# Decoder kernel: scan rows shared by two engines, paired spreads, residual at the first down products, low halves on GpSimd

## Time and profile before

| | us |
|---|---|
| time, median of 3 runs | 3944.65 |
| the profiled execution: its time, and its span | 3938.74, 3937.0 |
| PE busy, DVE busy | 3515.4 (89%), 3180.0 (81%) |
| ACT busy, POOL busy | 1623.4 (41%), 1347.1 (34%) |
| mean granted TensorE clock | 0.941 of full speed |

### The profile page before, as it was taken

How to read it: one execution, slowest core, us unless ns; L and a number is a source line. 1 busy time by engine, 2 the same in 40 slices (tenths; PEclk the granted TensorE clock), 3 DMA queues, 4 the chain that set the end, 5 groups by cost and what they waited for, 6 DMA issues and landing times. The chain is left out here.

```text
span 3937.0 us, 41370 instructions
## 1 busy us (share of the span) xinstructions
PE 3515.4 (89%) x15406; PEld 1471.1 (37%) x15406; DVE 3180.0 (81%) x2733; ACT 1623.4 (41%) x2201; POOL 1347.1 (34%) x493
## 2 busy tenths in 40 slices
PE   5777779989999979999999989998999989977998
PEld 1222243334333443334333443334433443324444
DVE  5999569888999869788999869888999869795333
ACT  5666343224655353224655343224655353213001
POOL 3455304362344304352344304352344304351000
PEclk9888899999899999989999999999899999988999
DMA  6678402221233302221233302221233302110322
GB/s 231 244 278 299 174 17 73 76 72 57 87 100 104 132 27 73 76 65 64 88 104 101 132 27 73 76 69 61 87 100 105 132 27 73 57 41 17 104 97 73
DMA packets 105430, 382.94 MB, mean 97 GB/s; under 512 B 14224, under 2 KB 27920, under 8 KB 102800
## 3 DMA queue, kind: packets, MB, share of 16 engines
q1 hardware_dynamic: 83632, 342.57, 25.5%
q10 hardware_dynamic: 21600, 37.73, 3.4%
HBM read 290.80 MB, written 64.32 MB: 90 GB/s over the span
## 5 line engine op out<-in xcount | busy, mean ns | idle before, releaser
L300 PE MATMUL ps<-r,ring 128*128 128x512 bf16 (+1 forms) x2040 | 780.8, 383 | 0.0
L297 PE MATMUL ps<-xr,ring 128*128 128x512 bf16 x1568 | 613.8, 391 | 0.3 <-PEq L1853 0.3
L301 PE MATMUL ps<-xr,ring 128*128 128x512 bf16 x1568 | 610.8, 390 | 0.0
L297 PE MATMUL ps<-r,ring 128*128 128x512 bf16 (+2 forms) x1384 | 546.8, 396 | 50.2 <-DVE xc L1107 17.9
L301 PE MATMUL ps<-r,ring 128*128 128x512 bf16 (+2 forms) x1384 | 545.5, 395 | 0.0
L1159 POOL TENSOR_TENSOR hh<-hh,bc 128x2048 f32<-128x2048 f32 x72 | 334.8, 4650 | 512.3 <-DVE hh L1069 512.3
L1159 POOL TENSOR_TENSOR bc<-bc 128x2048 f32<-128x2048 f32 x64 | 304.3, 4755 | 344.5 <-DVE bc L1069 344.5
L1159 POOL TENSOR_TENSOR r<-r,bc 128x2048 f32<-128x2048 f32 x56 | 261.3, 4667 | 298.5 <-DVE r L1069 298.5
L1069 DVE TENSOR_TENSOR_SCAN hh<-da,hh 128x2048 f32<-128x2048 f32 x72 | 325.6, 4523 | 1.2
L1110 DVE TENSOR_TENSOR xc<-xc,ps 128x512 f32<-128x512 f32 x176 | 119.5, 679 | 226.7 <-PE ps L301 226.7
L1069 DVE TENSOR_TENSOR_SCAN bc<-da,bc 128x2048 f32<-128x2048 f32 x64 | 296.3, 4630 | 0.5
(11 more groups left out here) (271 smaller groups left out, 6552.5 us busy)
## 6 DMA issues: line engine op xcount, KB each, us to landing
ring<-wsplit SPq DMA_DIRECT2D x216, 768.0 KB, 4.3
r<-wstream SPq DMA_DIRECT2D x54, 768.0 KB, 7.5
ring<-wsplit SPq DMA_DIRECT2D x76, 512.0 KB, 4.0
wsplit<-ring SPq DMA_DIRECT2D x38, 768.0 KB, 4.8
da<-r ACTq DMA_DIRECT2D x360, 63.9 KB, 2.1
wsplit<-r SPq DMA_DIRECT2D x14, 768.0 KB, 5.0
r<-wstream SPq DMA_DIRECT2D x19, 512.0 KB, 6.3
r<-xT SPq DMA_DIRECT2D x7, 1024.0 KB, 4.8
```

Source lines behind the costliest of these rows:

```text
L297: mm = pe.matmul(out, w_hi, x_hi, start=start, stop=False)
L300: pe.matmul(out, w_hi, x_lo, start=False, stop=False)
L301: return pe.matmul(out, w_lo, x_hi, start=False, stop=stop)
```

## The change

Four parts, in the words of the code:

- In the first scan (`halved`) POOL multiplies two of the four groups of a block with C, and DVE the other two, right after `inputs(step + 1)`. `reduce_quad` waits for both.
- In the expert stage every fourth spread of dt*x (`early_spread`: blocks 4, 8, ... 28) goes to `y_bank`, one step earlier, directly behind the spread of the block before it. `inputs_of` moves from `step % 4 == 2` to `step % 4 == 1`.
- In ffn and expert stages the first four down products are added to the residual `xr` instead of copied; ln2 and ln5 leave out `sums` and its wait.
- `ffn_xlo` is made by POOL at the end of `norm_and_steps`, a quarter after each quarter of `scaled`, instead of by DVE at the start of the ffn stage.

```diff
+        own_read, halved = sem("own_read"), not tiles
+        def early_spread(s):
+            return gated and s % 4 == 0 and 4 <= s < blocks
+        def input_bank(s):
+            return y_bank if early_spread(s) else dtx_bank
             def spread_dtx(s):
-                if s >= 1:
-                    pe.wait_ge(inp, s)
+                if early_spread(s):
+                    if s >= 8:
+                        pe.wait_ge(yout, s // 4 - 1)
+                elif s >= 1:
+                    pe.wait_ge(inp, s - 1 if early_spread(s - 1) else s)
...
-                pe.matmul(dtx_bank, k.headmean[at, :], source, start=True, stop=True).then_inc(dtx_mm, 1)
+                pe.matmul(input_bank(s), k.headmean[at, :], source, start=True, stop=True).then_inc(dtx_mm, 1)
             def reduce_quad(j):
                 pe.wait_ge(read, 4 * j + 4)
+                if early_spread(4 * j + 4):
+                    pe.wait_ge(inp, 4 * j + 5)
+                if halved:
+                    pe.wait_ge(own_read, 4 * j + 4)
...
-            if tiles and not gated:
-                pe.wait_ge(xsplit, KM)
...
-                if 2 <= step + 1 < blocks:
+                if 2 <= step + 1 < blocks and not early_spread(step + 1):
                     spread_dtx(step + 1)
+                if early_spread(step + 2):
+                    spread_dtx(step + 2)
...
-                    dve.tensor_copy(k.xc[:, m, :], down_bank(p)).then_inc(taken, 1)
+                    dve.tensor_tensor(k.xc[:, m, :], k.xr[:, m, :], down_bank(p), ALU.add).then_inc(taken, 1)
...
-            if tiles and not gated:
-                for c in range(KM):
-                    low(dve, xlo[:, c, :], k.xr[:, c, :]).then_inc(xsplit, 1)
...
+                if halved and step < blocks:
+                    dve.wait_ge(scanned, step + 1)
+                    own = quartet(step)[:, GRP // 2:GRP, :]
+                    dve.tensor_tensor(own, own, k.out_rows[:, GRP // 2:GRP, :], ALU.mult).then_inc(own_read, 1)
...
-                if which == 0 and step % 4 == 2 and step + 2 < blocks:
+                if which == 0 and step % 4 == (1 if gated else 2) and step // 4 * 4 + 4 < blocks:
                     inputs_of(step // 4 + 1)
...
-                pool.tensor_tensor(quartet(s), quartet(s), k.out_rows, ALU.mult).then_inc(read, 1)
+                rows = slice(0, GRP // 2 if halved else GRP)
+                pool.tensor_tensor(quartet(s)[:, rows, :], quartet(s)[:, rows, :], k.out_rows[:, rows, :], ALU.mult).then_inc(read, 1)
...
 class LayerNorm:
     def means(self, pe):
-                pe.wait_ge(self.res, 2 * h + c // 2 + 1)
+                if not self.summed:
+                    pe.wait_ge(self.res, 2 * h + c // 2 + 1)
     def sums(self, dve):
+        if self.summed:
+            return
...
 def norm_and_steps(...):
         def _(pool):
             s.build_spread(pool)
+            for half in range(2):
+                for pair in range(2):
+                    pool.wait_ge(norm.out, 2 * half + pair + 1)
+                    part = lambda region: region[:, 2 * pair:2 * pair + 2, half * HT:(half + 1) * HT]
+                    pool.tensor_tensor(part(k.ffn_xlo), part(k.xr), part(high(k.xr)), ALU.subtract)
```

More of the change, by code:

```diff
@@ L587, in second_preparation @@
         if store is not None:
-            norm = LayerNorm(k, "ln5", k.xc, k.xr, [k.ps[:, 6 + h, 0:HT] for h in range(2)], [k.ps[:, 6 + h, HT:T] for h in range(2)], True)
+            norm = LayerNorm(k, "ln5", k.xc, k.xr, [k.ps[:, 6 + h, 0:HT] for h in range(2)], [k.ps[:, 6 + h, HT:T] for h in range(2)], True, True)
         gates_in = k.dt0
@@ L819, in hidden_and_scan @@
         gate_mm, up_mm, th, silu, hid, weighted = [sem(n) for n in ("gate_mm", "up_mm", "th", "silu", "hid", "weighted")]
-        hidlo, xsplit, down, taken = [sem(n) for n in ("hidlo", "xsplit", "down", "taken")]
+        hidlo, down, taken = [sem(n) for n in ("hidlo", "down", "taken")]
         dt_mm, dtx_mm, decay, others = [sem(n) for n in ("dt_mm", "dtx_mm", "decay", "others")]
@@ L1058, in inputs @@
                     dve.wait_ge(reduced, (s - NB) // 4 + 1)
-                dve.tensor_tensor(quartet(s), dtx_bank[:, None, :].broadcast_to([P, GRP, T]), k.in_rows, ALU.mult).then_inc(inp, 1)
+                dve.tensor_tensor(quartet(s), input_bank(s)[:, None, :].broadcast_to([P, GRP, T]), k.in_rows, ALU.mult).then_inc(inp, 1)
             def inputs_of(j):
@@ L1158, in _, with __init__ @@
                 pool.wait_ge(scanned, s + 1)
-                pool.tensor_tensor(quartet(s), quartet(s), k.out_rows, ALU.mult).then_inc(read, 1)
+                rows = slice(0, GRP // 2 if halved else GRP)
+                pool.tensor_tensor(quartet(s)[:, rows, :], quartet(s)[:, rows, :], k.out_rows[:, rows, :], ALU.mult).then_inc(read, 1)
 class LayerNorm:
-    def __init__(self, k, tag, parts, residual, mean_bank, var_bank, shared=False):
+    def __init__(self, k, tag, parts, residual, mean_bank, var_bank, shared=False, summed=False):
+        self.summed = summed
         self.shared = shared
@@ L1235, in scaled, with layer_norm @@
                                   ALU.mult).then_inc(self.out, 1)
-def layer_norm(nc, k, tag, parts, slots_end, last, store=None, load=None, split=None, ranges=(), residual=None):
+def layer_norm(nc, k, tag, parts, slots_end, last, store=None, load=None, split=None, ranges=(), residual=None, summed=False):
     with ExitStack() as ctx:
@@ L1245, in layer_norm @@
         norm = LayerNorm(k, tag, parts, k.xr if residual is None else residual, [k.ps[:, 4 + h, 0:HT] for h in range(2)],
-                         [k.ps[:, 6 + h, 0:HT] for h in range(2)])
+                         [k.ps[:, 6 + h, 0:HT] for h in range(2)], summed=summed)
         blk = ctx.enter_context(nc.Block())
@@ L2355, in sequence @@
                     hidden_and_scan(nc, k, "ffn", FFN_TILES, W_FFN, 1, False, last, end=W_PROJ + 3 if ahead else None)
-                    layer_norm(nc, k, "ln2", k.xc, W_MIX, last, load=(k.xn, xT[b + 1]) if ahead else None,
+                    layer_norm(nc, k, "ln2", k.xc, W_MIX, last, summed=True, load=(k.xn, xT[b + 1]) if ahead else None,
                                split=k.xn_lo if ahead else None)
@@ L2364, in sequence @@
                     if not ahead:
-                        layer_norm(nc, k, "ln5", k.xc, last, last, store=out[b])
+                        layer_norm(nc, k, "ln5", k.xc, last, last, store=out[b], summed=True)
                 if ahead:
```

## The result

The changed kernel takes a median of 3919.68 us in four runs (3912.42 to 3927.57), the kernel before 3946.62 beside it: ratio 0.9937, 95% interval 0.9918 to 0.9957. Measured a second time it takes 3922.38 us beside 3941.38 for the kernel before: 0.9947 (0.9929 to 0.9966). (Times are medians; the ratios are worked out from all runs, so they differ a little from the quotient of two medians.) The forecast was 3908, with 3890 to 3931: the time lies inside, 12 us above the forecast. By its parts, two terms came out as forecast and two brought about half and 0.6 of it.

A forecast was written before the change was run, and what follows sets the result against it. It took the first scan as bound by DVE's and POOL's SBUF work end to end, the expert stage by PE with DVE close behind. Terms -20 - 23 - 4 + 10 = -37 us gave 3908 us from the median, range 3890 to 3931.

The forecast's parts named there:

- First scan: First scan, 32 blocks: POOL's multiply shared with DVE shortens each block; -20 us, bounds -31 and +5.
- 32 x 1.1 is 35 us: First scan: a gain of 1.1 us read in single blocks, taken for all 32, 35 us before deductions.
- The third taken off for what is late next: First scan: the 30 us gain cut by a third because weight loads would not shrink with the steps, leaving -20 us.
- The rival in which the split leaves only 4 us: First scan: the weight split bounds it, so it gains 4 us instead of 20; 3924 us, chance 0.20.
- Paired spreads: Three expert stages, seven pairs each: two spreads cost PE the time of one; 3 x 7.6 = -23 us, bounds -29 and 0.
- each of the six waits falls by 1.05 and by what PE was ahead: Expert stage: DVE's six waits for a spread, 9.8 us, shrink to 2.2 us, saving 7.6 us a stage.
- the slower rival: Expert stages: the early spread stops PE at the wait for `inputs_of` in every quad, +136 us; 4067 us, chance 0.04.
- the one in which pairs bring little: Expert stages: the two matmuls don't run side by side, or DVE limits at once; -3 for -23, 3928 us, chance 0.10.
- Residual: Four ln2 and the last ln5: without `sums` PE's means start about 0.75 us sooner; -4 us, bounds -1 and -7.
- Low halves: Four ln1 stages: POOL's instructions exclude DVE's last six, 2.5 us longer each; +10 us, bounds 0 and +14.
- the rival in which they are free: ln1: POOL's four instructions fall into gaps of DVE and cost nothing; 3898 us, chance 0.05.

The follow-up runs named there:

- short loads: The changed kernel with each load of weights in the first scan cut to 384 of up to 1536 columns, output not the reference's: 3916.64 us in one execution.
- the gap filled: The changed kernel with ffn_xlo's low halves back on DVE, plus 32 useless matmuls at the end of PE's order in ln1: 3916.15 us, ratio 0.9926.

## Why the prediction was right, and where its terms were not

**First scan: -20 forecast, -10.5 measured** (327 to 330 us against 337 to 340; -11.7 in the profiled execution). What it said of the single block holds. The changed kernel's timeline:

```profile
295.58 2.36 POOL L1176 TENSOR_TENSOR hh<-hh,bc 128x1024 f32<-128x1024 f32 x1 [6.13 <-DVE hh L1084]
...
298.94 4.41 DVE L1084 TENSOR_TENSOR_SCAN bc<-da,bc 128x2048 f32<-128x2048 f32 x1
303.28 1.73 DVE L265 TENSOR_TENSOR r<-r 128x1536 bf16<-128x1536 f32 x1
303.43 3.79 POOL L1176 TENSOR_TENSOR bc<-bc 128x1024 f32<-128x1024 f32 x1 [5.49 <-DVE bc L1084]
305.07 2.29 DVE L1074 TENSOR_TENSOR bc<-ps,bc 128x2048 f32<-128x2048 f32 x1
307.28 1.22 DVE L1142 TENSOR_TENSOR bc<-bc 128x1024 f32<-128x1024 f32 x1
308.41 4.42 DVE L1084 TENSOR_TENSOR_SCAN bc<-da,bc 128x2048 f32<-128x2048 f32 x1
```

From scan to scan (298.94 to 308.41) it is 9.47 us with a piece of low half, 9.33 forecast, and 7.85 without one (144.14 to 151.99), 7.68 forecast; scans take 4.41 throughout. By the Trainium skill (SBUF — State Buffer, section "SBUF: two separate sides") DVE with two inputs in SBUF and POOL exclude each other for a whole instruction; the trace agrees, since POOL's half takes 3.79 us behind line 265 and 2.36 at 295.58, where DVE is in `inputs`.

The step that failed is "32 x 1.1 is 35 us": it carried a pattern read in two blocks to all. There are 31 intervals from the end of one scan to the end of the next. Taken one by one in the two traces, 20 of them are 1.0 us shorter (0.98 to 1.03); the other eleven are together 9.7 us longer. With 1.1 us that the tail gains, as forecast, this is the 11.7.

Two things are in the eleven. The first is work. In the trace of before, DVE stands behind POOL's multiply in 28 of the 31 intervals, but not always in the scan: 18 of the 32 scans are longer than 5.5 us; seven times line 1063 in front of a scan took the wait (2.80 to 3.05 us in place of 0.68), and three times line 265 did (here 5.36 and 3.98 us in place of 1.73). In three intervals nothing did, since DVE had waited for its spread until POOL was done or nearly so, as here from 284.95:

```profile
284.95 2.29 DVE L1059 TENSOR_TENSOR hh<-ps,bc 128x2048 f32<-128x2048 f32 x1 [3.91 <-PE ps L894]
287.81 4.42 DVE L1069 TENSOR_TENSOR_SCAN hh<-da,hh 128x2048 f32<-128x2048 f32 x1
343.19 5.36 DVE L265 TENSOR_TENSOR ring<-r,ring 128x1536 bf16<-128x1536 f32 x1 [0.86 <-ACT ring L260]
357.55 3.98 DVE L265 TENSOR_TENSOR ring<-r,ring 128x1536 bf16<-128x1536 f32 x1 [2.27 <-ACT ring L260]
```

In those three the own half adds 1.1 us and removes nothing. 28 x 1.0 - 3 x 1.1 is 25 us in place of 35. `finish_y` was hidden in three of its eight blocks only (before scans of 6.15, 5.80 and 6.15 us), so it costs 2 and not 5, and the own half of the last block costs DVE another 1.2: 22 us of DVE's work, with 21.3 measured, where the forecast had 30. The second is waits, below. The groups of the stage (count, busy, mean ns, idle before) show the trade. Before:

```profile
L1069 DVE TENSOR_TENSOR_SCAN bc<-da,bc 128x2048 f32<-128x2048 f32 x10 | 58.1, 5807 | 0.5
L265 DVE TENSOR_TENSOR ring<-r,ring 128x1536 bf16<-128x1536 f32 (+3 forms) x16 | 33.6, 2100 | 3.9 <-ACT ring L260 3.9
L1063 DVE TENSOR_TENSOR ctxTs<-r 128x512 f32<-128x512 f32 x8 | 20.8, 2606 | 0.3 <-PEq L486 0.3
```

After:

```profile
L1084 DVE TENSOR_TENSOR_SCAN bc<-da,bc 128x2048 f32<-128x2048 f32 x10 | 44.1, 4412 | 0.0
L1074 DVE TENSOR_TENSOR hh<-ps,bc 128x2048 f32<-128x2048 f32 x12 | 27.4, 2286 | 18.9 <-PE ps L905 18.9
L265 DVE TENSOR_TENSOR ring<-r,ring 128x1536 bf16<-128x1536 f32 (+3 forms) x16 | 25.9, 1621 | 10.6 <-ACT ring L260 10.6
L1078 DVE TENSOR_TENSOR ctxTs<-r 128x512 f32<-128x512 f32 x8 | 5.5, 682 | 0.3 <-PEq L486 0.3
L1142 DVE TENSOR_TENSOR bc<-bc 128x1024 f32<-128x1024 f32 x10 | 12.1, 1210 | 0.0
```

DVE's busy time falls by 21.3 us (312.39 to 291.09) and its idle time grows by 9.6: waits for the spread 12.5 to 19.6 us, for ACT's half of the split 3.9 to 10.6, for the reduction 8.4 to 6.0. Five intervals lose 1.4 to 3.4 us each by them, three to the spread and two to ACT. The third taken off for what is late next (10 us) was thus right in size, and 21.3 less 9.6 is the 11.7. The loads are a part of it (short loads: 3 to 7 us); how the rest divides between PE's order and ACT wasn't settled, except that the bank of the spread isn't it. The rival in which the split leaves only 4 us holds in part: DVE's waits for ACT's half grew by 6.7 us, but ACT's own waits for loads, which it named, fell from 9.1 + 2.4 us to 6.3 + 2.1.

**Paired spreads: -23 forecast, -13.8 measured** (4.8, 4.4 and 4.7). A pair costs 1.06 us as the earlier trace rows said, here from 1183.43 to the product behind it:

```profile
1183.43 1.13 PE L905 MATMUL ps<-ctxTs,squares_sb 32*128 32x512 f32 x4 [0.15 <-issue]
1184.49 0.40 PE L297 MATMUL ps<-xr,ring 128*128 128x512 bf16 x1
```

and PE's four steps take 40.07 us, 40.1 forecast. The failing step is "each of the six waits falls by 1.05 and by what PE was ahead". DVE's waits after the first blocks are now

```profile
DVE r L1074 <- PE ps L905: 2.4, 2, 1.2
DVE hh L1074 <- PE ps L905: 1.4, 2, 0.9
DVE bc L1074 <- PE ps L905: 1.0, 2, 0.5
```

4.8 us, not 2.2, for 9.8: a fall of 5.0, the stage's own. The lead doesn't add up from quad to quad: at its start PE must wait for DVE (8.2 us of waits), and what two pairs save there is handed back at once. Only pairs behind which PE is the limit count: five, 5 x 1.05 = 5.3 with 4.6 seen on average. The new wait for `inputs_of` stops PE once, 4.1 us, in place of the old 5.0, as said; it stops no later quad, so the slower rival (4067 us) has nothing for it. Nor has the one in which pairs bring little.

**Residual: -4 forecast, -3.9 measured** (5 x 0.8); the second preparation stays at 41.1 us.

**Low halves: +10 forecast, +9.2 measured** (4 x 2.3). DVE's busy time grows by 3.16 us (17.58 to 20.74), 3.4 forecast, less 0.86 of idle time; the rival in which they are free is off. In ffn nothing comes back: DVE's first `inputs` is 3.9 us behind the start, as before, now after an idle time of 4.09 us.

**The sum** is -19.0 by stage, -37 forecast: half of it. The medians give -27 in the first measurement and -19 in the second. So the forecast's time was nearer than its terms, and that the first measurement came within 12 us of it is in part luck: 8 us of its 27 are not found in the stages that the change touches. The mechanisms (the lock, the pair, the earlier means, the lock again in ln1) are those that the runs show; the sizes of the two large terms were not.

## What to carry to other kernels

Before a saving in one loop step is multiplied by the number of steps, count the steps in which the cause that it removes was really the last to end. One row per step of the instruction that showed it first isn't enough (here the scan, 4.4 or 6.4 us, shows 18 of 28): the same wait can fall on any instruction of that engine that needs the lock, so look at each one's time against its time alone. Work given to the limiting engine costs in every step, and pays only where the lock held it. A faster engine that is ahead anyway hands its lead back at the next single buffer, so a saving on it counts only in the stretches in which others wait for it. A cure for two engines that exclude each other is another time: POOL's low halves cost 2.3 us in ln1 and nearly nothing at the start of the next stage. That kernel took 3899.78 us in its one execution, in which no ln1 met the low clock; by stages some 9 us of what it is under the changed kernel are this edit's. Leaving the low halves on DVE brings the same 9 us by stages (3913.62 and 3917.14 us in twelve executions, 3902.85 the shortest), and nothing here tells the two apart. Either, with the three other parts, is the version to go on with.

## What had not been expected of the hardware

- A small instruction can pay several times its own length for the lock: line 1063 (128x512, two SBUF inputs) took 2.6 us on average in the first scan of before, mostly behind POOL, and takes 0.68 now.
- Instructions of DVE and POOL that follow each other closely take turns: DVE's 128x512 took 1.49 us each beside POOL's, POOL's 1.64.
- The same ln1 takes 23.6 or 26.8 us without POOL's part, as its means fall on the higher clock or in part on the lower (mean clock 0.86 or 0.74 in the stage), and once 28.4 (0.69). After 7.27 us in which PE did nothing the clock was low for the first spreads (2.04 us for one, 1.09 with the gap filled).
